# Four layers of a block on one core: VectorE reads one input from PSUM, a second bias moves to GpSimd, inverse denominators are transposed, an expert's layers wait for their own weights

## What is computed

```python
# 1: y = norm(x); sliding-window attention (16 heads of 16, window 128), then an MLP of 1024; out = y
q, k, v = split(ln1(y) @ w_qkv.T); y = y + (softmax(mask(q @ k.T)) @ v) @ w_o.T
y = y + gelu(ln2(y) @ mlp_w1.T + b1) @ mlp_w2.T + b2
# 2: token mix (x_prev is x shifted by one token)
xr, xk = mu_r*x + (1-mu_r)*x_prev, mu_k*x + (1-mu_k)*x_prev
out = sigmoid(xr @ W_r) * (square(relu(xk @ W_k)) @ W_v)
# 3: selective scan
xp, z = split(x @ in_w.T); xc = silu(causal_conv(xp, 4 taps))
dt, B, C = split(xc @ x_w.T); delta = softplus(dt @ dt_w.T + dt_b)
h[t] = exp(delta[t]*A) * h[t-1] + delta[t]*B[t]*xc[t]          # 512 channels x 16 states
out = ((sum_n h*C + D*xc) * silu(z)) @ out_w.T
# 4: one of 8 experts per sequence, chosen by the mean token
out = relu(x @ W1[e] + b1[e]) @ W2[e] + b2[e]
```

## Time and profile before

| | |
|---|---|
| median of three runs | 3789.12 us (3778.06 to 3798.62) |
| profiled execution | 3792.8 us, its span 3790.9 us |
| busy: TensorE, VectorE, ScalarE, GpSimd | 3120.8, 2831.7, 2403.9, 2860.8 us |
| TensorE's mean granted clock | 0.911 of full speed |
| moved by DMA | 735.6 MB, mean 194 GB/s |

### The profile page before, as it was taken

The page is one execution under the profiler, slowest core; times in us unless marked ns, Lnnn a source line. Parts: engine busy times, 40 slices in busy tenths (PEclk is TensorE's granted clock), DMA queues, the critical chain, the costliest instruction groups (busy, mean ns, idle before and its releaser), DMA issues.

```text
span 3790.9 us, 58550 instructions
## 1 busy us (share of the span) xinstructions
PE 3120.8 (82%) x17648; PEld 1915.7 (51%) x17648; DVE 2831.7 (75%) x6080; ACT 2403.9 (63%) x5299; POOL 2860.8 (75%) x2511
## 2 busy tenths in 40 slices
PE   5878788887988989798898979889797988977457
PEld 3545354453645546465464636555464654644235
DVE  3357878787787878878787877778788787879860
ACT  5567667575767757676675857667576766754331
POOL 1118889887888879887897978888798878977770
PEclk9998888898999999899898989989998998988678
DMA  2026777777777778776877867787787768789980
GB/s 70 6 78 182 195 193 201 202 206 211 190 209 224 190 216 210 229 196 182 232 212 208 219 200 207 194 225 188 220 213 227 203 185 232 210 241 242 254 224 34
DMA packets 422204, 735.60 MB, mean 194 GB/s; under 512 B 53306, under 2 KB 99010, under 8 KB 421890
## 3 DMA queue, kind: packets, MB, share of 16 engines
q1 hardware_dynamic: 421890, 731.85, 70.7%
HBM read 647.80 MB, written 83.89 MB: 193 GB/s over the span
## 4 chain that ended last, share of the span: by engine, by line
PE 52%; DVE 16%; POOL 10%; ACT 9%; issue 8%; DMA 3%; SPq 1%; DVEq 0%; ACTq 0%; POOLq 0%
PE bank L454 13%; PE bank L462 8%; PE bank L577 6%; PE bank L720 5%; POOL u_rows L1455 5%; PE bank L487 5%; DVE u_rows L1266 4%; POOL u_rows L1448 4%; PE bank L499 4%; PE bank L656 4%; PE bank L708 3%; DMA u_rows<-u_dram 3%; PE bank L515 2%; ACT prob L775 2%; DVE region_b L1198 1%
## 5 line engine op out<-in xcount | busy, mean ns | idle before, releaser
L1455 POOL TENSOR_TENSOR u_rows<-u_rows,c_rows 128x512 f32<-128x512 f32 x1024 | 1339.1, 1311 | 261.9 <-DVE state L1271 208.3
L1448 POOL TENSOR_TENSOR u_rows<-u_rows,b_rows 128x512 f32<-128x512 f32 x960 | 1275.0, 1329 | 33.0 <-DMA u_rows<-u_dram 32.7
L938 ACT ACTIVATE bank<-d_rows,a_rep 128x512 f32<-128x512 f32 x1024 | 697.7, 689 | 283.7 <-DMA d_rows<-delta_dram 127.1
L1266 DVE TENSOR_TENSOR_SCAN u_rows<-bank,state,u_rows 128x512 f32<-128x512 f32 x512 | 642.6, 1270 | 67.6 <-ACT bank L938 64.6
L1266 DVE TENSOR_TENSOR_SCAN u_rows<-bank,u_rows 128x512 f32<-128x512 f32 x512 | 622.7, 1216 | 62.9 <-ACT bank L938 60.4
L656 PE MATMUL bank<-u_rows,sum_n 128*32 128x512 f32 x2048 | 307.1, 674 | 310.3 <-POOL u_rows L1455 303.6
L775 ACT ACTIVATE prob<-prob,neg_max 128x256 f32<-128x256 f32 x1024 | 511.6, 507 | 40.7 <-DVE neg_max L1050 40.4
L1050 DVE CUSTOM_DVE_ANT_0 prob<-bank,band 128x256 f32<-128x256 f32 x896 | 336.9, 416 | 145.5 <-PE bank L487 117.0
L499 PE MATMUL bank<-ident,prob 128*128 128x128 f32 x2048 | 332.4, 290 | 107.2 <-ACT prob L775 66.7
L499 PEld LDWEIGHTS bank<-ident,prob 128*128 128x128 f32 x2048 | 243.1, 147 | 265.0 <-issue 192.1
L487 PE MATMUL bank<-kT,q_own 32*128 32x256 f32 x2048 | 304.3, 417 | 46.4 <-DVE neg_max L1050 26.6
(11 more groups left out here) (163 smaller groups left out, 5661.6 us busy)
## 6 DMA issues: line engine op xcount, KB each, us to landing
u_rows<-u_dram SPq DMA_DIRECT2D x1024, 256.0 KB, 5.5
d_rows<-delta_dram SPq DMA_DIRECT2D x1024, 256.0 KB, 5.3
w<-in_W SPq DMA_DIRECT2D x28, 1024.0 KB
zs_dram<-region_b SPq DMA_DIRECT2D x64, 256.0 KB, 2.2
xc_dram<-region_b SPq DMA_DIRECT2D x64, 256.0 KB, 2.5
delta_dram<-region_b SPq DMA_DIRECT2D x64, 256.0 KB, 2.8
u_dram<-region_b SPq DMA_DIRECT2D x64, 256.0 KB, 2.1
yg<-xc_dram SPq DMA_DIRECT2D x64, 256.0 KB, 5.0
```

The source lines that it names most:

```text
L938: e.activation(banks[at.bank][:, :], delta_of(i, k), ACT.Exp, scale=a_rep[:, j:j + 1]).then_inc(filled[at.bank], 1)
L1266: e.tensor_tensor_scan(rows, banks[at.bank][:, :], rows, state[:, k:k + 1] if i % 2 else 0.0, ALU.mult, ALU.add).then_inc(drained[at.bank], 1)
L1448: e.tensor_tensor(rows, rows, b_rows[:, :], ALU.mult).then_inc(bx_ready.sem, 1)
L1455: e.tensor_tensor(rows, rows, c_rows[:, :], ALU.mult).then_inc(hc_ready.sem, 1)
```

## The change

VectorE's operations with two inputs in SBUF take one of them from a PSUM bank: the mix from the transposed bank, the squaring, the gates, the residual, delta's maximum and the u product; four kinds write their result into the bank they read. ScalarE copies delta from the bank to SBUF for the store, which now comes after u's. The edge columns of the convolution are computed by GpSimd in even groups and added once. The bias of the expert's second layer is broadcast to all partitions, added to the residual by GpSimd, and no longer a product. The inverse denominators are turned by a transposition. W1 with b1, and W2 with b2, have a semaphore each. Banks are held longer accordingly.

```diff
-        return [("t3.0", 0, 1), ("t3.1", 0, 1), ("rk0", 4, 5), ("rk1", 6, 7), ...
+        return [("t3.0", 0, 2), ("t3.1", 0, 3), ("rk0", 4, 6), ("rk1", 6, 8), ...
-                + [(f"dt{m}", 18 + 2 * m, 19 + 2 * m) for m in range(4)])
+                + [(f"dt{m}", 18 + 2 * m, 22 + 2 * m) for m in range(4)])
...
 # pe_attention, values_of
-                e.matmul(banks[at.bank][:, P:2 * P], rden_wide[:, k * P:(k + 1) * P], ident[:, :],
-                         start=True, stop=True).then_inc(filled[at.bank], 1)
+                e.transpose(banks[at.bank][:, P:2 * P], rden_wide[:, k * P:(k + 1) * P],
+                            ident[:, :]).then_inc(filled[at.bank], 1)
...
 # pe_expert
-            e.wait_ge(*picked(i))
+            e.wait_ge(*w1_there(i))
...
+                if half == 0:
+                    e.wait_ge(*w2_there(i))
...
-                    e.matmul(out, ones_row[:, :], e_b2[:, :], start=False, stop=True).then_inc(filled[at.bank], 1)
...
 # act_rwkv
-            act_transposed(e, (use("t3.0"), use("t3.1")), norm_b)
...
-                    e.activation(mixT[:, a, k, :], nb[:, k, 0:G], ACT.Copy, scale=col[mu][:, k:k + 1]).then_inc(mix_half.sem, 1)
+                    e.activation(mixT[:, a, k, 1:G], banks[at.bank][:, 0:G - 1], ACT.Copy,
+                                 scale=col[mu][:, k:k + 1]).then_inc(mix_half.sem, 1)
...
 # act_middle, after the exp and log of tile m
+            def copy_delta(m):
+                at = use(f"dt{m}")
+                e.wait_ge(*u_ready.at(i, m + 1))
+                e.wait_ge(*zs_stored[m].at(i))
+                e.activation(delta[:, m, :], banks[at.bank][:, :], ACT.Copy).then_inc(drained[at.bank], 1)
+                if m:
+                    copy_delta(m - 1)
...
 # dve_rwkv
-                    e.scalar_tensor_tensor(out=mixT[:, a, k, :], in0=nb[:, k, 1:1 + G], scalar=col[mu][:, k:k + 1],
+                    ins = e.scalar_tensor_tensor(out=mixT[:, a, k, :], in0=banks[at.bank][:, :], scalar=col[mu][:, k:k + 1],
...
-                e.tensor_tensor(kT2[:, m, :], kT2[:, m, :], kT2[:, m, :], ALU.mult).then_inc(k_sq.sem, 1)
+                e.scalar_tensor_tensor(out=kT2[:, m, :], in0=banks[at.bank][:, :], scalar=0.0, in1=kT2[:, m, :],
+                                       op0=ALU.max, op1=ALU.mult).then_inc(drained[at.bank], 1)
...
+                e.scalar_tensor_tensor(out=xs, in0=banks[at.bank][:, :], scalar=0.5, in1=xs,
+                                       op0=ALU.mult, op1=ALU.add).then_inc(drained[at.bank], 1)
...
 # dve_middle
-                        e.scalar_tensor_tensor(out=xc[:, m, 0:n], in0=xp_tail[:, m, TAPS - 1 - n:TAPS - 1], scalar=tap,
-                                               in1=xc[:, m, 0:n], op0=ALU.mult, op1=ALU.add).then_inc(edge.sem, 1)
+                if g and m == KE - 1:
...
+                    e.tensor_tensor(xc[:, :, 0:TAPS - 1], xc[:, :, 0:TAPS - 1], edge_rows[:, :, :], ALU.add).then_inc(edge.sem, 1)
...
-                e.tensor_scalar(delta[:, m, :], banks[at.bank][:, :], col["dt_b"][:, m:m + 1], None,
-                                ALU.add).then_inc(drained[at.bank], 1)
...
-                e.tensor_tensor(delta[:, m, :], delta[:, m, :], norm_b(m % 2), ALU.max).then_inc(delta_ready.sem, 1)
+                e.scalar_tensor_tensor(out=banks[at.bank][:, :], in0=banks[at.bank][:, :], scalar=col["dt_b"][:, m:m + 1],
+                                       in1=norm_b(m % 2), op0=ALU.add, op1=ALU.max).then_inc(delta_formed.sem, 1)
...
-                e.tensor_tensor(xc[:, m, :], delta[:, m, :], xc[:, m, :], ALU.mult).then_inc(u_ready.sem, 1)
+                e.tensor_tensor(xc[:, m, :], banks[at.bank][:, :], xc[:, m, :], ALU.mult).then_inc(u_ready.sem, 1)
...
                 low_in(m)
-                yield
-                yield
-                if m == KE - 1:
-                    low_out(m)
-                    yield
-                else:
-                    low_out(m)
+                if m:
+                    low_out(m - 1)
+                yield
+                yield
+            low_out(KE - 1)
...
 # dve_scan, gate
-                e.scalar_tensor_tensor(out=yg[:, m, :], in0=yg[:, m, :], scalar=0.5, in1=zg[:, :],
+                e.scalar_tensor_tensor(out=yg[:, m, :], in0=banks[at.bank][:, :], scalar=0.5, in1=zg[:, :],
...
 # pool_rwkv, ahead of its first step
+            e.wait_ge(*full(uses["mlp", i, "m3"]))
+            if g == 0:
+                ins = e.memset(mixT[:, :, :, 0:1], 0.0)
+            else:
+                e.wait_ge(*gone(uses["rwkv", i - 1, "t3.1"]))
+                ins = e.tensor_tensor(mixT[:, :, :, 0], last_n[:, :, :].rearrange("p k o -> p o k").broadcast_to([P, 2, KD]),
+                                      not_mu.rearrange("p (a k) -> p a k", a=2), ALU.mult)
...
 # pool_middle, step 13 of even groups: five operations of up to 128x12
+                e.wait_ge(*tail_ready.at(i // 2, KE))
+                e.tensor_tensor(edge_rows[:, :, :], xp_tail[:, :, :], tap(0, TAPS - 1), ALU.mult)
...
 # pool_expert, step 7 of 25
+            e.wait_ge(*w2_there(i))
+            e.wait_ge(*ln_c.out.at(i, 1))
+            e.tensor_tensor(xs, xs, e_b2[:, :].rearrange("p (o c) -> p o c", o=1).broadcast_to([P, GT, D]),
+                            ALU.add).then_inc(b2_added.sem, 1)
...
 # sp_middle, store_delta
-                e.wait_ge(*delta_ready.at(i, m + 1))
-                e.dma_start(delta_dram[i % 2, m * P:(m + 1) * P, :], delta[:, m, :]).then_inc(d_stored[m].sem, 16)
                 e.wait_ge(*u_ready.at(i, m + 1))
                 e.dma_start(u_dram[i % 2, m * P:(m + 1) * P, :], xc[:, m, :]).then_inc(u_stored[m].sem, 16)
+                e.wait_ge(*gone(uses["middle", i, f"dt{m}"]))
+                e.dma_start(delta_dram[i % 2, m * P:(m + 1) * P, :], delta[:, m, :]).then_inc(d_stored[m].sem, 16)
...
 # sp_fetch: W1, b1, b2 (now broadcast to all partitions), W2; one semaphore for W1 and b1, one for b2 and W2
```

More of the change, by code:

```diff
@@ L596, in pe_rwkv @@
                 yield
-            e.wait_ge(*mix_ready.at(i, 4))
+            e.wait_ge(*gone(use("t3.0")))
+            e.wait_ge(*gone(use("t3.1")))
             for n in range(GT // 2):
@@ L601, in pe_rwkv @@
                 yield
-            e.wait_ge(*k_sq.at(i, 2))
+            e.wait_ge(*gone(use("rk0")))
+            e.wait_ge(*gone(use("rk1")))
             for n in range(GT // 2):
@@ L675, in pe_back @@
             yield
-            e.wait_ge(*yg_ready.at(i, KE))
+            e.wait_ge(*gone(uses["scan", i, "y3"]))
             for n in range(GT // 2):
@@ L1168, in dve_rwkv @@
                     yield
-            for n in range(GT // 2):
-                xs = tiles(x1[:, g, :, :], n)
-                e.wait_ge(*gone(use(f"rv{n}")))
-                e.scalar_tensor_tensor(out=xs, in0=tiles(zb, n), scalar=0.5, in1=xs,
-                                       op0=ALU.mult, op1=ALU.add).then_inc(x2_ready.sem, 1)
             yield
-            e.wait_ge(*x2_ready.at(i, 2))
+            e.wait_ge(*gone(use("rv0")))
+            e.wait_ge(*gone(use("rv1")))
             dve_stats(e, ln_b, i, 1, x1[:, g, :, :])
@@ L1204, in convolution @@
                         e.wait_ge(*taps.at(i, 2 * m + n))
-                        if g:
-                            e.wait_ge(*edge.at(i // 2, 3 * m + n))
                 ins.then_inc(drained[at.bank], 1)
+                if g and m == KE - 1:
+                    for n in range(KE):
+                        e.wait_ge(*gone(use(f"x{n}")))
+                    e.wait_ge(*edge_sum.at(i // 2, 3))
+                    e.tensor_tensor(xc[:, :, 0:TAPS - 1], xc[:, :, 0:TAPS - 1], edge_rows[:, :, :], ALU.add).then_inc(edge.sem, 1)
             def gate(m):
```

166 lines of the change are left out of this document (98 added, 68 removed).

## The result

The changed kernel takes 3616.02 us, median of four runs (3610.29 to 3620.18), against 3793.87 us of the kernel before (four runs, 3778.06 to 3801.57). The ratio is 0.9537, 95% interval [0.9519, 0.9556]: 4.6% faster, some 176 us. The forecast was 3609. The profiled execution took 3620.18 us, with a span of 3618.1.

The account below looks back on a forecast made before the run. It took TensorE as the bound for most of a step, VectorE and GpSimd together in two places. Gains of 156 us in the middle, 8 in the head and the rest at the ends, 180 together, gave 3609 us, range 3535 to 3715.

Parts of the forecast that it names:

- the head: Start of the run: 3 us gained from the turns and 5 in its own delta stage, 8 us.
- the middle: The 13.8 steady pipeline steps: 11.3 us gained in each, 156 us.
- the two parts of the tail: From 3420 to 3660 us, 8 from faster arithmetic; at the end, 3 from earlier weights and 5 from removed bias products.
- VectorE's saving: Over the run, inputs moved to PSUM, fewer edge operations and a dropped dt copy save VectorE 276 us, 17 a step.
- The stalls: Waits on VectorE in each step: 5.5 us less in the delta stage and 2.5 in the token mix.
- rival 2: Delta stage: the DMA engines take back its gain, 5.5 us a step lost; 3685 us, chance 0.10.
- rival 3: Held dt banks and the later delta store delay scan and row loads, 13.3 us a step; slower, 3822 us, chance 0.06.
- The edges: Convolution's edge operations in odd steps, where one of 5.38 us stood on the chain: 1.7 us a step gained.
- TensorE: 3.6 a step: Removed bias products (2.5) and shorter turns (1.7), counted where TensorE is the bound: 3.6 us a step gained.
- the charge of 2.0: GpSimd's second-bias addition near the full stretch hides TensorE's gain: 2.0 us a step lost.
- (1): GpSimd becomes the bound in the steps, losing TensorE's gain and half of the stalls'; 3699 us, chance 0.13.
- (4): VectorE's slow operations have another cause than input place, such as semaphores, and stay slow; 3699 us, chance 0.05.

Follow-up runs that it names:

- the tensor half: Turns as transpositions, second bias added by GpSimd, separate waits for the two layers' weights; alone on the kernel before: 1.0048 of its time.
- e4: Changed kernel with six kinds of VectorE operation reading both inputs from SBUF again, waits and banks kept; 0.9828 of the kernel before.
- e9: Changed kernel with only delta's maximum and the u product reading both inputs from SBUF; 0.9631 of the kernel before.
- e10: Changed kernel with VectorE's second copy of dt put back; 0.9619 of the kernel before.
- e8: Changed kernel with the edge columns computed by VectorE's 96 small operations again; 0.9744 of the kernel before.
- e3: Changed kernel with the turns, GpSimd's second bias and the separate weight waits undone; 0.9643 of the kernel before.
- e6: Changed kernel without GpSimd's addition of the second bias; 0.9521 of the kernel before.
- e1: Kernel before with only the turns of the inverse denominators made transpositions; 1.0004 of the kernel before.
- e2: Kernel before with the turns as transpositions, the second bias added by GpSimd and separate waits for weights; 1.0048 of the kernel before.
- e5: Kernel before with the 64 bias products of the expert's second layer left out; 0.9932 of the kernel before.
- e7: Changed kernel with GpSimd's addition of the second bias made twice; 0.957 of the kernel before.
- e11: Changed kernel with the normalisation's two small operations moved from VectorE to GpSimd; 0.9625 of the kernel before.

## Why the prediction was right, and which steps were not

**The sum.** Between the spans lie 172.9 us. The first product by c comes 4.0 us later than before (296.1 for 292.1), the 15 distances between first products are shorter by 161.1, and what follows the last is shorter by 15.8. The forecast had 8 for the head, 156 for the middle and 16 for the two parts of the tail. The total was right to 7 us and the middle to 5, and that is in part luck: the terms inside a step were off and offset one another, and so did the head and the middle. Undone one at a time they are 1.7 and 1.9 in the delta stage, 4.3 for the other inputs, 4.9 for the edges and 2.0 for the tensor half: 14.8 together against the 10.7 of all. A part undone brings a bound back that holds the others' gains too, so these prices are not a sum. The range was narrower than its own bounds: stalls of 4, TensorE's 3 and a charge of 4 leave 3 us a step, and with the 24 at the ends 65 us, not 100.

**The mechanism: right.** e4 shows it with nothing but the addresses of operands. VectorE's saving was 248.5 us against 276. By the groups of lines, the parts that the forecast names fell by 292 us. Against them stand the normalisation's small operations, which got slower: 192 of them took 60.1 us before and 88.1 after (the first kind, for `rstd_b`, a mean of 737 ns where it had 392). The forecast had left them out. The rest is small: other groups, and overlaps of rows, which the busy time counts once. Writing into PSUM cost nothing, as taken: 736 ns for the 728 of the same addition into SBUF. Of the two prices for reading PSUM, the rows' held and not the Trainium skill's ("VectorE: DVE Perf Modes", the section on the errata of trn2): the u product from a bank has a lowest of 690 ns and from SBUF, in e4, 691.

**The stalls: 8.0 a step forecast, near it as a sum, wrong in their places.** e9 and e10 together give the delta stage 3.6 us a step, for 5.5. The other four kinds have the rest of e4's 6.0, 4.3 a step, for 2.5. The split is approximate. TensorE's wait in the delta stage is 9.2, for a forecast of 8; "what is late next is GpSimd" holds (18.62 of 19 us). What the forecast had not seen is the wait for `nb` just behind it, 4.73 us (rivals 2 and 3, below).

**The edges: the term that was mis-sized.** The step said "TensorE had stood still for 3 to 4 of it: 1.7 a step"; e8 shows 4.9. It counted TensorE's own idle time and not GpSimd's 4.66 us right behind, which came through VectorE's queue. In the odd steps of e8 the two waits, 4.18 and 4.66 us, add up to 8.8 of the 9.3 us that these steps are longer than after's; that they are added in full is likely and not shown apart. The trace of before had both waits, behind its operation of 5.38 us:

```profile
1737.77 0.66 PE L499 MATMUL bank<-ident,prob 128*128 128x128 f32 x4 [3.43 <-DVE region_b L1200]
...
1739.87 1.26 POOL L1455 TENSOR_TENSOR u_rows<-u_rows,c_rows 128x512 f32<-128x512 f32 x1 [4.66 <-DVE state L1271]
```

It also had a clearer sign: of steps 3 to 14 its odd ones took 225 us and its even ones 218. They differ in other things too (the form of the scan, the routing), but after the change they are alike, 211.5 and 210.6.

**TensorE: 3.6 a step forecast; 2.0 measured, net of GpSimd's share.** e3 and after give 2.0 for the tensor half; the forecast had 3.6 - 2.0 = 1.6. But the parts are wrong: e6 refutes the charge of 2.0, so the gross gain is 2.3 and not 3.6. One part of the gap is a reading: the turn of the earlier trace rows with 0.42 us to the next start is no typical one; the median of all is 0.325, so the turns were worth 1.3 a step and not 1.7. Where the rest goes is in keeping with e1 and e3: shorter work returns in part as time at the lower clock. The forecast's other silence is the reverse of it: it took the stalls for idle time alone, while of the 10.7 us only 5.3 are idle time. TensorE's work fell by 5.4 a step; the instructions taken away are 3.8 of it, and the other 1.6 can't be traced with a granted clock of 0.93 in both kernels: that stays open. In e3, with no instruction gone, the work had fallen by 3.5 at a clock of 0.95. That "the bias lands near the full stretch, where GpSimd has no room" fell with the stretch itself: by undoing the stalls the change gave GpSimd's queue that room. In the kernel before it had none: there the addition cost some 44 us (e2 against e1 and e5).

**Rivals.** (1) GpSimd as the bound: no, by e6, but near, by e7 and e11. (2) The DMA engines, and (3) the row loads: in part. They did take back some of the delta stage's gain, in the one place where ScalarE waits 4.10 us for a row of delta for 1.50: the wait for `nb` behind it grew by 33 us over the run (63.9 for 30.6), some 2 us a step. The forecast had put it at nothing ("row loads wait for free buffers rather than run late"). It isn't the 5.5 of rival 2 nor the 13.3 of rival 3, and no wait for delta's banks is in the list. Whether the row is late because its load stands behind the later store or because the same bytes are packed closer was not tried. (4) fell with e4.

**The head and the end.** The head did not gain its 8 us. The turns are shorter there too, but TensorE's clock was 0.89 and 0.90 in the two halves of the first 292 us against 0.95 and 0.93 before, and it was busy 218.1 us against 213.7. One profile says little here: e4 and e10, which differ from after only in VectorE's inputs or one copy, have 0.94 in their first 291 us and reach the first product by c at 290.9 and 291.5. Even so, no kernel run here is more than 1.2 us ahead of before's 292.1. The end went as forecast: the last wait for weights fell from 9.77 to 6.80 us (3 forecast), and from its end to that of the span are 67.3 us instead of 72.0 (5 forecast).

## What to carry to other kernels

Where VectorE and GpSimd run side by side, look at the spread of each VectorE operation's durations (lowest, median, highest) rather than at its mean: a form that has both inputs in SBUF and at times lasts two to thirty times its lowest value was cured here by reading one input from a bank that already held it. Price such a stall by what stands in the queues behind it on every engine, and compare steps that have the operation with steps that have not; one engine's own idle time gave a third of the real price. Work moved to another engine is priced by what that engine can spare at the time: GpSimd's additions cost some 44 us while the stalls were there and 6, within the error, once they were gone, so that the same edits lost 18 us before and brought 40 after.

## What the runs showed of the hardware that was not expected

- **Less work for TensorE can come with more time at the lower clock.** e1 takes some 20 us of matmuls away, and its time stays the same, with 735 us at the lower clock for 697 by the medians of 12 and 23 runs; e2's median clock of 0.892 over 10 runs makes some 820. That the clock is all of the reason is not shown. In the kernel after, the clock falls where the engine stands still: 0.96 in a stretch with 43.5 of 47 us busy, 0.82 with 9.8 of 19, 0.69 in the one after it.
- **A blocked VectorE operation can wait for several of GpSimd's instructions in a row.** In e8 the one-column operation starts at 1689.42 and ends at 1695.38, and GpSimd, without a gap, ends six instructions in that time, the last at 1694.10 + 1.27 = 1695.37. The Trainium skill ("SBUF — State Buffer", who interferes with whom) has the later engine blocked until the other's instruction ends, 1.3 us here; these rows show more than four times that.
- **Neither a small size nor a single input protects.** Of the two operations on 128 x 4 values, each with one tensor input in SBUF, the first reaches 4.56 us for a lowest of 0.17, while the reciprocal on 128 x 8 (mean 198 ns, highest 204) and the copy of one column (144 and 156) beside the same products do not stall.
